# MLP layer of a four-layer fp32 kernel: rounded values transposed by DMA, w1 product in row tiles

## What is computed

```
x = x + L0(gn(x));  x = x + L1(gn(x));  x = x + L2(gn(x));  x = x + L3(gn(x))

def quantize_rowwise(x):
    scale = clip(max(|x|, axis=-1), 1e-12) / 448.0
    return (x / scale).astype(float8_e4m3fn), scale
def fp8_linear(x, w):
    xq, sx = quantize_rowwise(x);  wq, sw = quantize_rowwise(w)
    return (xq @ wq.T) * sx * sw.T

# L2, for every token (64 channels)
h = layer_norm(x) * ln_w + ln_b
a, b = split(fp8_linear(h, w1), 2)      # w1: 512 x 64, so a and b have 256 values
out = fp8_linear(relu(a) * b, w2)       # w2: 64 x 256
```

## Time and profile before

| | |
|---|---|
| three runs | 1978.09, 1988.72, 1985.76 us; median 1985.76 |
| profiled execution | 1991.03 us, span of the trace 1989.2 us |
| stage A of layer 2 | from 902 to 1146 us of the span |
| stage B of layer 2 | from 1146 to 1606 us |
| busy over the span | DVE 1630.4 us (82%), PE 1505.3 (76%), ACT 1251.1 (63%), POOL 1028.4 (52%) |

### The profile page before, as it was taken

How to read it: one execution, slowest core, us unless ns; L and a number is a source line. 1 busy time by engine, 2 the same in 40 slices (tenths; PEclk the granted TensorE clock), 3 DMA queues, 4 the chain that set the end, 5 groups by cost and what they waited for, 6 DMA issues and landing times.

```text
span 1989.2 us, 31133 instructions
## 1 busy us (share of the span) xinstructions
PE 1505.3 (76%) x9710; PEld 975.6 (49%) x9744; DVE 1630.4 (82%) x4038; ACT 1251.1 (63%) x2571; POOL 1028.4 (52%) x730
## 2 busy tenths in 40 slices
PE   5479999798799987981111288888888859998775
PEld 1156668564566685650111124444443437776664
DVE  6899961897999717978999958999989979992488
ACT  2256641896455517974566658777787837772488
POOL 7288830685888406867676501222222268870254
PEclk8789999899899998995555558989899889999869
DMA  6034443676344345771111001111111124435377
GB/s 235 11 85 106 107 103 90 182 198 202 85 107 106 81 122 160 212 201 59 38 42 43 22 0 33 43 43 43 43 44 47 50 80 112 111 91 133 104 233 252
DMA packets 314373, 201.96 MB, mean 102 GB/s; under 512 B 248992, under 2 KB 249312, under 8 KB 314208
## 3 DMA queue, kind: packets, MB, share of 16 engines
q1 hardware_dynamic: 175776, 162.21, 28.0%
q10 hardware_dynamic: 138432, 37.76, 8.1%
HBM read 114.97 MB, written 66.06 MB: 91 GB/s over the span
## 4 chain that ended last, share of the span: by engine, by line
issue 37%; PE 28%; DVE 14%; ACT 9%; POOL 6%; DMA 4%; SPq 0%; ACTq 0%; DVEq 0%; POOLq 0%
PE ps L1088 10%; ACT work L935 7%; PE ps L1093 6%; PE ps L1049 4%; PE ps L1078 4%; PE ps L1168 4%; DMA gate_dram<-work 3%; POOL work L445 3%; POOL work L491 2%; DVE stats L671 2%; ACT work L921 2%; DVE ln_s L687 1%; DVE work L592 1%; DVE pairs L789 1%; DVE pairs L757 1%
## 5 line engine op out<-in xcount | busy, mean ns | idle before, releaser
L485 POOL TENSOR_TENSOR ln_s<-ln_s,half_power 128x8 f32<-128x8 f32 x252 | 417.6, 1657 | 373.3 <-DVE ln_s L680 317.4
L1088 PE MATMUL ps<-work 128*128 128x384 f32 x864 | 319.5, 493 | 3.5 <-ACT work L921 3.5
L1049 PE MATMUL ps<-work,ones 128*128 128x512 f32 x504 | 282.3, 677 | 27.0 <-ACT work L897 17.8
L946 ACT ACTIVATE work<-ps 128x768 f32<-128x768 f32 x216 | 175.1, 811 | 175.0 <-DMA gate_dram<-work 141.2
L935 ACT ACTIVATE work<-pairs,ln_s 128x64 f32<-128x64 f32 x648 | 263.0, 493 | 17.8 <-DVE ln_s L687 17.8
L491 POOL TENSOR_TENSOR work<-pairs,work 128x512 f32<-128x512 f32 x36 | 47.5, 1320 | 372.8 <-DVE pairs L855 372.8
L1093 PE MATMUL ps<-work 128*128 128x256 f32 x864 | 223.4, 381 | 0.0
L477 POOL TENSOR_TENSOR work<-work,gn_rstd 128x512 f32<-128x512 f32 x144 | 185.1, 1286 | 62.4 <-DVE work L636 56.9
L1093 PEld LDWEIGHTS ps<-work 128*128 128x128 f32 x864 | 165.7, 192 | 69.6 <-issue 1.8
L1179 PE MATMUL ps<-ident,pairs 128*64 128x128 bf16 x576 | 38.8, 312 | 201.9 <-DVE pairs L789 201.0
L1088 PEld LDWEIGHTS ps<-work 128*128 128x128 f32 x864 | 156.8, 192 | 70.3 <-ACT work L921 6.9
(11 more groups left out here) (131 smaller groups left out, 3189.5 us busy)
## 6 DMA issues: line engine op xcount, KB each, us to landing
work<-x_mid SPq DMA_DIRECT2D x144, 256.0 KB, 2.7
gate_dram<-work ACTq DMA_DIRECT2D x108, 256.0 KB, 3.1
work<-gate_dram SPq DMA_DIRECT2D x108, 256.0 KB, 3.1
work<-in_x_in SPq DMA_DIRECT2D x72, 256.0 KB, 2.8
work<-x_nat SPq DMA_DIRECT2D x144, 128.0 KB, 3.0
x_mid<-work SPq DMA_DIRECT2D x72, 256.0 KB, 2.1
work<-pairs SPq DMA_DIRECT2D x96, 96.0 KB, 3.0
work<-pairs ACTq DMA_DIRECT2D x96, 96.0 KB, 3.1
```

The costliest lines, as they stand in the source:

```text
L485: pool.tensor_tensor(ln_s[:, b, RSTD, :], ln_s[:, b, VAR, :], half_power[:, 0:U], ALU.pow)\
L946: act.activation(sig[:, b, :].rearrange("p (k g) -> p k g", k=PAIRS)[:, 2 * half:2 * half + 2, :], ps[:, bank:bank + 2, 0:GATES], ACT.Sigm ...
L1049: last = pe.matmul(ps[:, bank, :], ones[:], src[:, b, :], start=first, stop=end, skip_group_check=True)
L1088: last = pe.matmul(ps[:, GATE_BANK[half] + k, 0:GATES], xnT[:, b, (2 * half + k) * P:(2 * half + k + 1) * P], wpair[:, VALUES:VALUES + GAT ...
```

## The change

In stage A and stage B the transposes leave PE and ACT: SP issues a DMA transpose per tile, `q_in` to `q_all` (128 x 512 bf16) and `q_hid` to `q_hidT` (128 x 2048 bf16). A tile of 128 x 128 holds two tokens of 64 channels one under the other, so `hidden_layer` works on a pair at once: token 0 on rows 0 to 63 of the array and token 1 on rows 64 to 127, each against the first part of w1 (512 columns) and the second and third (256 columns each, the a half alone). The w1 preparation multiplies the a half by both row scales (a's and b's) and leaves the b half as its rounded values. `square_sx` is gone from DVE; ACT squares all `sx` once between the stages. `hidden_row_scale` writes straight to `sg_all`, so a copy is gone. Orders change on DVE, ACT, PE and SP.

```diff
-        q_all = wide[:, 17408:17408 + TILES * ROW].bitcast(BF16).rearrange("p (t f) -> p t f", t=TILES)
+        q_all = wide[:, 17408:17408 + TILES * ROW // 2].bitcast(BF16).rearrange("p (t k n) -> p t k n", t=TILES, k=PAIRS)
...
+            def transpose_q(t, b):
+                sp.wait_ge(hq_ready, t + 1)
+                sp.dma_start_transpose(q_all[:, t, :, :], q_in[:, b, :]).then_inc(qT_ready[b], 16)
+
+            def transpose_hidden(t, b):
+                sp.wait_ge(hid_q, 2 * (t + 1))
+                wait_free(sp, mlp_out_ready, t - 1)
+                sp.dma_start_transpose(q_hidT[:, b, :, :], q_hid[:, b, :]).then_inc(hqT_ready[b], 16)
...
-                    pipeline(sp, [(0, lambda t, b: load_x(l, t, b, False))])
-                    pipeline(sp, [(1, lambda t, b: load_residual_mlp(l, t, b)),
-                                  (0, lambda t, b: store_x(l, t, b, False))])
+                    pipeline(sp, [(6, lambda t, b: load_x(l, t, b, False)),
+                                  (-1, transpose_q)])
+                    pipeline(sp, [(-5, lambda t, b: load_residual_mlp(l, t, b)),
+                                  (-6, lambda t, b: store_x(l, t, b, False)),
+                                  (-3, transpose_hidden)])
...
-            chain(by_row_scale(wq_y, wq_q, 1), 9)
+            dve.tensor_tensor(wscale[:, 1, 0:2], wscale[:, 1, 0:2], wscale[:, 1, 2:4], ALU.mult).then_inc(s_wscale, 1)
+            dve.wait_ge(s_wscale, 1)
+            for j in range(2):
+                dve.tensor_scalar(wq_y[:, j * P:(j + 1) * P], wq_q[:, j * P:(j + 1) * P], wscale[:, 1, j:j + 1], None, ALU.mult)
+            dve.tensor_copy(wq_y[:, 2 * P:4 * P], wq_q[:, 2 * P:4 * P])
...
-                wait_free(dve, qT_psum, t - 1)
+                wait_free(dve, qT_ready[b], 16 * (t // 2))
...
-            def square_sx(t, b):
-                wait_free(dve, hid_step, 6 * t)
-                dve.tensor_tensor(tok[:, 4, :], tile_row(sx_all, t), tile_row(sx_all, t), ALU.mult).then_inc(hid_step, 1)
...
-                dve.tensor_copy(tile_row(sg_all, t), tok[:, 6, :])
-                dve.reciprocal(tok[:, 7, :], tok[:, 6, :]).then_inc(hid_step, 1)
+                dve.wait_ge(hid_step, 5 * t + 3)
+                dve.reciprocal(tok[:, 7, :], sg_all[:, t, :]).then_inc(hid_step, 1)
...
                     pipeline(dve, [pair(0), (-6, lambda t, b: mlp_update(l, t, b)),
-                                   pair(1), (-1, square_sx), (-1, hidden_amax, RING), add(0), (-1, amax_of_product),
-                                   pair(2), round_(0), (-1, hidden_row_scale), add(1), (-1, hidden_inverse),
+                                   add(0), pair(1), (-1, hidden_amax, RING),
+                                   pair(2), (-1, amax_of_product), round_(0), (-1, hidden_row_scale), add(1), (-1, hidden_inverse),
                                    pair(3), (-1, hidden_rescale), round_(1)])
...
+                    act.wait_ge(h_step, 3 * TILES)
+                    act.activation(sx2_all[:], sx_all[:], ACT.Square).then_inc(sx2_ready, 1)
...
                     pipeline(act, [pair(0), scale(0),
-                                   pair(1), scale(1),
-                                   pair(2), evacuate(0), absolute(0), (-6, lambda t, b: square(sum_base(l) + t, b)),
-                                   pair(3), evacuate(1), absolute(1)])
+                                   pair(1), absolute(0),
+                                   pair(2), scale(1),
+                                   pair(3), absolute(1), (-6, lambda t, b: square(sum_base(l) + t, b))])
...
-                for h in range(2):
-                    out_ab = ps[:, 2 * (pp % 2) + h, :]
-                    u = 2 * pp + h
-                    q_token = q_all[:, bass.ds(t, 1), u * P:(u + 1) * P].rearrange("p o n -> p (o n)")
-                    pe.matmul(out_ab, q_token, w1s[:, 0, :], start=True, stop=False)
-                    last = pe.matmul(out_ab, q_token[0:C], w1s[0:C, 2, :], start=False, stop=True)
+                for part_, width in enumerate((2 * HID, HID, HID)):
+                    for h in range(2):
+                        rows = slice(C * h, C * h + C)
+                        last = pe.matmul(ps[:, 2 * (pp % 2) + h, 0:width], q_all[rows, t, pp, :], w1s[rows, part_, 0:width],
+                                         start=part_ == 0, stop=part_ == 2, skip_group_check=True)
...
-                    pipeline(pe, [pair(0), pair(1), sums(SUM), turn(0), out_half(0),
-                                  pair(2), sums(SQ), pair(3), turn(1), out_half(1)])
+                    pipeline(pe, [pair(0), sums(SUM), pair(1), out_half(0),
+                                  pair(2), sums(SQ), pair(3), out_half(1)])
```

More of the change, by code:

```diff
@@ L881, in _ @@
                                    (5, lambda t, b, r: centre(l, t, b, r), RING)])
-                    dve.wait_ge(qT_ready, TILES)
+                    for b in range(2):
+                        dve.wait_ge(qT_ready[b], 8 * TILES)
                     pair = lambda pp: (0, lambda t, b, r: hidden_product(pp, t, b, r), RING)
@@ L1170, in project_out @@
                 last.then_inc(out_ready, 1)
-            def transpose_q(t, b):
-                pe.wait_ge(hq_ready, t + 1)
-                wait_free(pe, qT_ready, t - 1)
-                pe.sem_inc(s_pe_apart, 1)
-                for u in range(U):
-                    for copy in range(2):
-                        last = pe.transpose(ps[copy * C:copy * C + C, T_BANK + b, :].bitcast(BF16)[:, u * P:(u + 1) * P],
-                                            q_in[:, b, u * C:(u + 1) * C], ident16[:])
-                last.then_inc(qT_psum, 1)
@@ L1183, in hidden_layer @@
             def hidden_layer(pp, t, b):
[L1186 to L1187 removed]
+                if t == 0 and pp == 0:
+                    for parity in range(2):
+                        pe.wait_ge(qT_ready[parity], 8 * TILES)
                 k = PAIRS * t + pp
                 wait_free(pe, acc_used, k - 1)
[L1190 to L1195 removed]
@@ L1196, in hidden_layer @@
-                last.then_inc(acc_ready, 1)
-            def transpose_hidden(half, t, b):
-                pe.wait_ge(hid_q, 2 * t + half + 1)
-                wait_free(pe, hqT_ready, 2 * t + half)
-                for k in range(8):
-                    last = pe.transpose(ps[:, H_BANK, :].bitcast(BF16)[:, k * P:(k + 1) * P],
-                                        q_hid[:, b, (8 * half + k) * P:(8 * half + k + 1) * P], ident16[:])
-                last.then_inc(hqT_psum, 1)
+                for part_, width in enumerate((2 * HID, HID, HID)):
[3 more added lines that the diff above has]
+                                         start=part_ == 0, stop=part_ == 2, skip_group_check=True)
@@ L1212, in mlp_out @@
                         for chunk in range(2):
-                            last = pe.matmul(ps[:, O_BANK, u * C:(u + 1) * C], q_hidT[:, b, (2 * u + chunk) * P:(2 * u + chunk + 1) * P],
+                            last = pe.matmul(ps[:, O_BANK, u * C:(u + 1) * C], q_hidT[:, b, 2 * u + chunk, :],
                                              w2s[:, part_, chunk * C:(chunk + 1) * C],
```

77 lines of the change are left out of this document (30 added, 47 removed).

## The result

The changed kernel takes 1912.58 us (median of 4 runs, 1910.86 to 1918.34), the kernel before 1986.15 (4 runs): ratio 0.9641, 95% interval 0.9607 to 0.9675, 73.6 us less. 1911 was forecast.

What follows compares the result with a forecast made beforehand. DVE was taken as the bound in stages A and B. Savings of 63 + 11 + 0.5 = 74.5 us from 1991.0 gave 1916.5, or 1911 us beside the median; forecast's own range 1897 to 1932, 8-in-10 range 1892 to 1990.

Steps and rivals of the forecast that it cites:

- Steady step: Stage B: a step falls from 12.24 to 10.07 us; thirty steps at 2.1 us each save 63 us.
- `square_sx` 0.93: DVE's step in stage B: removing the 8-element square, which stood behind POOL's shift_new, gains 0.93 us.
- the addition and the copy: DVE's stage B step: first-half hidden_add before the second pair's product gains 1.14 us; one 8-element copy gone, 0.1.
- Parts 4 and 5: Steady stage B: two evacuations off ACT and 16 transposes off PE, and the new w1 product, each worth 0.
- The cover named: Steady stage B: DVE's 10 us hides the w1 product; without that cover the product would be a gain only.
- The lock (rival C): Moved add against POOL's update_mlp: DVE first, cost 0; rival: POOL first, 1947 us, chance 0.08 including smaller new waits.
- First steps: Start of stage B, at PE's lower clock: row tiles cut 60.8 us to 49.4, saving 11 us.
- DMA transposes (rival A): SP's transposes: latency of 3 to 10 us hidden; rival: they can't keep up, 2124 us at 16 a tile, chance 0.21.
- The seam: Between stage A's last rounding and stage B: the DMA transpose's landing time of 3.0 us costs 0.
- Rival B: Steady stage B: PE stays at the lower clock and bounds, 11.7 us a step, 1960 us; chance 0.08.
- Drain: End of stage B, transposes issued two short steps ahead: 0 to 1 us gained, 0.5 taken.

Runs made afterwards that it cites:

- the last experiment: Changed kernel with three reorderings: POOL's bias first, DVE's h_amax ahead of ln_shift and ln_var, residual load before the transpose on SP; 1905.13 us, ratio 0.9580.

## Why the prediction was right, point by point

- **Steady step, 12.24 to 10.07, 63 us.** 10.09 and 61.4. The terms of DVE's list hold, in the order in which the prediction takes them and in steps with PE at the higher clock: `square_sx` 0.93 (12.22 to 11.29, forecast 0.93), then the addition and the copy 1.20 (11.29 to 10.09, forecast 1.14 and 0.1). They depend on each other, which the prediction didn't say: with the addition moved first it is worth 1.44 and the squares 0.49, as POOL then holds up `square_sx` for a shorter time.
- **Parts 4 and 5, "0" in the steady step.** This is the step of the reasoning that failed: wrong as to their worth. The cover named, "DVE's 10 us", isn't there if the PE work stays: with the transposes on PE the step is 10.60, with the old product as well 12.09 in the new order. "without that cover it would be a gain only" saw it from the old list; the question was whether the old PE work fits under the new one. It doesn't: from rows at the lower clock a step then needs 4 x 2.18 (w1) + 2 x 2.13 (a turn and a w2 half, 1403.77 to 1405.90) + 2 x 2.0 (sums) = 17.0 us of PE, with the new product 12.1 (that run's longest steps are 12.0), and without the transposes 4 x 0.97 + 2 x 1.39 + 2 x 2.0 = 10.7. No step of 17.0 exists, since none is wholly at the lower clock; the longest with the old product are 13.8, with about half of the w1 matmuls there. At the higher clock the old list is 9.3 us and would fit. The same low stretches are why each DVE edit alone gave less than its term (mean steps 0.27 and 0.32 us above the commonest, 8 and 9 us in 29 steps). That the bundle came out at its sum is owed to the two parts that were booked at 0.
- **The lock (rival C).** As forecast: 1.21 for the addition, 2.18 for POOL, the same in all steps from 1240 to 1500.
- **First steps, 60.8 to 49.4.** 48.9. A pair takes 0.97 us (1.18 forecast) against 2.18, a ratio of 0.44 where the earlier trace rows gave 0.55.
- **DMA transposes (rival A).** 4.3 us to land, inside the 3 to 10 that were hidden, and 2.75 us of throughput. Within the steps of stage B neither DVE nor PE waits for one. The Trainium skill (VectorE: DVE Perf Modes, The three transpose paths) gives 1309 ns for a block of 128 x 128, as an estimate 21 us a tile if added up: the trace disagrees, 16 blocks in one instruction take 2.75. Its 261 GB/s (DMA: Bandwidth & Descriptors, Latency and other measured facts), 2 us a tile as an estimate, is nearer: 512 KB in 2.75 us are 191 GB/s, 27% less.
- **The seam, "0".** PE's first product of stage B is released by the last transpose, and yet the time from the last rounding of stage A to DVE's first product fell from 7.24 to 5.04 us. The new w1 product with its layout of the rounded values brought that (3.97 us when put in alone, with the transposes on PE); the DMA transpose costs 1.1 of it.
- **Rival B.** Granted clock 0.91 in the steady window, as before. PE's rows at the lower level appear in it (1.04), yet hardly an interval shows them: all but one of the 29 are 10.1, one is 10.4.
- **Drain, "0 to 1 us gained, 0.5 taken".** 1.4 lost. The `mlp_update` at 1527.25 waits 5.06 us, last for the residual's load, which stands behind a transpose in SP's queue; but PE's w2 product before it (1525.43 + 1.49 = 1526.92) ends only 0.33 us sooner. Loading the residual earlier gave a drain of 31.0 in one run and of 32.0 in the other: in the first PE's product ran at the higher clock (0.86 us), in the second at the lower (1.49). So the load is worth 0.3 us at most, and the rest of the 1.4 stays open.

Left open: the steady step with both DVE edits on the old PE lists, the transposes by DMA put in alone, and why the ratio of the last experiment gained more than its stage.

## What to carry to other kernels

Time that an instruction stands behind another engine belongs to the place in the order, not to the instruction: before removing or moving one, ask which comes next and whether it would stand too. If it wouldn't (here a reduction or a product out of PSUM), the whole time is won; if it would, little. When the bound engine's list gets shorter, price the other engines' whole list at the lower clock, with what is queued behind each of their waits, against the new step; edits worth 10, 14 and 29 us alone were, with the transposes, worth 73 together. An edit that gives little alone may be a condition for the next. And read a run's steps one by one: a mean of 11.56 was thirteen steps of 11.3, which were as forecast, and eight of 12.6, which named what was missing.

## What the runs showed of the hardware

- A small DVE instruction with a single SBUF input and a constant stood behind POOL too: `ln_var`, 128 x 8, 0.54 us instead of 0.16 in `ln_s<-stats` above, until POOL's L489 ended at 1012.10. I had expected that only of two inputs. The reduction (0.67 at all times) and products out of PSUM didn't. The Trainium skill (SBUF — State Buffer, Summary: rules for kernel authors) names both cases, two SBUF inputs and a 2-port mode, and says that the later one fully blocks; the trace agrees that it stands, and can't say whether `ln_var` ran in a 2-port mode.
- Matmuls of 64 rows on the two halves of the array overlap two by two (84.2 us of them in 43.1 of busy time), and they need not alternate: 0.61 and 1.04 us for six in either order.
- SP is held 1.9 us (median) by issuing one 128 x 2048 transpose and 2.75 when several follow each other, so a load behind it in that queue starts late.
